# Local attention with its probabilities normalised before the transposition, and its output produced already transposed

## The reference, cut to what matters

```python
qkv = x @ Wqkv; q, k, v = split into 16 heads of 64
q = rotary(l2norm(q) * qs); k = rotary(l2norm(k) * ksc)
# windows of 64 tokens; each sees itself and the window before it: 64 queries x 128 keys
sim = einsum('bhwie,bhwje->bhwij', bq, bk2) * 8.0
sim = where(mask, -max, sim)
attn = softmax(sim, -1)
out = einsum('bhwij,bhwje->bhwie', attn, bv2)
x = x + out.transpose(0, 2, 1, 3).reshape(b, n, 1024) @ Wo
x = x + ffn_layer(x)            # layer norm, 256 -> 2 x 682 with a gelu gate -> 256
```

## Time and profile before

| | |
|---|---|
| median of 3 runs | 5769.8 us (5769.42 to 5777.96) |
| profiled execution | 5762.77 us, its span 5761.5 us |
| mean granted TensorE clock | 0.952 |
| PE busy | 5043.6 us (88%) |
| PEld busy | 3178.3 us (55%) |
| DVE busy | 3618.7 us (63%) |
| ACT busy | 3127.5 us (54%) |
| POOL busy | 2235.3 us (39%) |

### The profile page before, as it was taken

How to read it: one execution, slowest core, us unless ns; L and a number is a source line. 1 busy time by engine, 2 the same in 40 slices (tenths; PEclk the granted TensorE clock), 3 DMA queues, 4 the chain that set the end, 5 groups by cost and what they waited for, 6 DMA issues and landing times.

```text
span 5761.5 us, 93567 instructions
## 1 busy us (share of the span) xinstructions
PE 5043.6 (88%) x36184; PEld 3178.3 (55%) x36184; DVE 3618.7 (63%) x6534; ACT 3127.5 (54%) x6626; POOL 2235.3 (39%) x2178
## 2 busy tenths in 40 slices
PE   5888889978887788877999999999999999999997
PEld 2223333334343343226777777777777777777775
DVE  4655466575665757656766666666666666666664
ACT  2554455433343334446766666666666666666662
POOL 1111001101010110108666666666666666666652
PEclk7999999989898899998999999999999999999998
DMA  4322232221221222211000000000000000000000
GB/s 97 52 48 53 40 56 50 51 52 37 54 40 38 37 50 42 50 20 56 9 16 18 18 21 20 22 16 19 20 16 23 16 22 16 23 16 16 23 9 30
DMA packets 125067, 189.04 MB, mean 33 GB/s; under 512 B 18800, under 2 KB 67568, under 8 KB 124400
## 3 DMA queue, kind: packets, MB, share of 16 engines
q1 hardware_dynamic: 124624, 183.06, 14.4%
HBM read 150.09 MB, written 32.51 MB: 32 GB/s over the span
## 4 chain that ended last, share of the span: by engine, by line
PE 60%; DVE 21%; ACT 10%; issue 6%; DMA 1%; POOL 1%; SPq 0%; DVEq 0%; ACTq 0%; POOLq 0%
PE psum L1206 15%; PE psum L1249 7%; PE psum L465 6%; PE psum L428 4%; PE psum L1250 3%; PE psum L449 3%; DVE maxes L651 3%; ACT probs L831 2%; DVE small_stats L1406 2%; PE psum L410 2%; ACT lprobs L1518 2%; PE psum L1258 2%; PE psum L1291 2%; ACT lwork L1493 2%; PE psum L1282 2%
## 5 line engine op out<-in xcount | busy, mean ns | idle before, releaser
L831 ACT ACTIVATE probs<-psum 128x1024 f32<-128x1024 f32 x768 | 766.7, 1019 | 674.9 <-PE psum L449 389.1
L651 DVE TENSOR_REDUCE maxes<-psum 128x1 f32<-128x1024 f32 x512 | 614.7, 1212 | 341.7 <-PE psum L428 337.8
L1393 DVE TENSOR_TENSOR lwork<-psum,rotary 128x512 f32<-128x512 f32 x384 | 265.2, 691 | 797.3 <-ACT lwork L1493 797.2
L1518 ACT ACTIVATE lprobs<-psum,small_stats,stats 128x128 f32<-128x128 f32 x1536 | 578.4, 459 | 334.3 <-DVE small_stats L1410 333.4
L1572 POOL TENSOR_TENSOR stats<-stats,minus_half 128x8 f32<-128x8 f32 x384 | 642.0, 1672 | 32.0
L1568 POOL TENSOR_TENSOR lwork<-lwork 128x512 f32<-128x512 f32 x384 | 492.2, 1282 | 368.5 <-DVE lwork L1395 364.4
L428 PE MATMUL psum<-stack 96*128 96x512 bf16 x1536 | 486.2, 400 | 152.7 <-ACT probs L831 121.5
L449 PE MATMUL psum<-stack 98*128 98x512 bf16 x1536 | 522.7, 396 | 107.1 <-DVE maxes L651 57.3
L930 POOL TENSOR_TENSOR attn<-attn,sums 128x512 f32<-128x512 f32 x48 | 60.8, 1267 | 1319.1 <-DVE sums L684 1319.1
L1493 ACT ACTIVATE lwork<-psum 128x512 f32<-128x512 f32 x384 | 232.1, 604 | 433.6 <-PE psum L1250 432.9
L1249 PE MATMUL psum<-wqkv_hi,xs_hi 128*128 128x512 f32 x768 | 345.8, 450 | 117.8 <-DVE att_lo L1424 73.5
(11 more groups left out here) (227 smaller groups left out, 12629.2 us busy)
## 6 DMA issues: line engine op xcount, KB each, us to landing
stack<-k_parts SPq DMA_DIRECT2D x288, 128.0 KB
staged<-in_quads SPq DMA_DIRECT2D x144, 256.0 KB, 2.5
k_parts<-parts SPq DMA_DIRECT2D x48, 384.0 KB, 2.8
stack<-q_parts SPq DMA_DIRECT2D x288, 64.0 KB
staged<-in_w SPq DMA_DIRECT2D x54, 256.0 KB, 2.7
ctx<-in_ctxT SPq DMA_DIRECT2D x24, 512.0 KB, 4.8
q_parts<-parts SPq DMA_DIRECT2D x24, 384.0 KB, 2.8
arena<-in_ctxT SPq DMA_DIRECT2D x8, 512.0 KB, 4.5
```

The lines of the kernel that those rows point to most:

```text
L651: ins = vector.tensor_reduce(to, pair(("M", u)), AX.XY, ALU.max)
L831: scalar.activation(probs[:, i % 6, :, :], pair(("E", u)), ACT.Exp).then_inc(S_["E_act"], 1)
L1518: ins = scalar.activation(pr[:, h, :], scores(u)[:, h % 2, h // 2, :], ACT.Exp, bias=st[:, 4 + h:5 + h], scale=y[:, h:h + 1])
```

## The change

Sums of the exponentials are taken by ScalarE while it makes them (`accum_out`). A new stage `nm` (lag 5) takes their reciprocals and multiplies the probabilities on VectorE, before they are turned. `pt` moves to lag 6 and `pv` to lag 7. In `pv` the values are now the weights and the turned probabilities move, so that features come out on the partitions, two heads of a pair in the two halves; `ot` and `heads_out` are gone, and ScalarE and VectorE split `pv`'s bank into `att_hi` and `att_lo`. The column of ones is gone. The maxima are written to PSUM, beside the scores, and read there. `probs` has 3 buffers, `vals` 7, `mixed_vals` 8.

```diff
-        for stage, lag in (("qkv", 0), ("rot", 1), ("tr", 3), ("sc", 4), ("ex", 4), ("pt", 5), ("pv", 6), ("ot", 7)):
+        for stage, lag in (("qkv", 0), ("rot", 1), ("tr", 3), ("sc", 4), ("ex", 4), ("nm", 5), ("pt", 6), ("pv", 7)):
-    rank = {st: i for i, st in enumerate(("wo", "sc", "tr", "rot", "ot", "pv", "ex", "pt"))}
+    rank = {st: i for i, st in enumerate(("wo", "sc", "nm", "tr", "rot", "pv", "ex", "pt"))}
...
                     for h in range(4):
+                        pair, e = h // 2, h % 2
                         for w in range(2):
-                            ins = tensor.matmul(bank(("pv", u, 0))[64 * w:64 * w + 64, h * (LHD + 1):(h + 1) * (LHD + 1)],
-                                                pt[:, h, 64 * w:64 * w + 64], (va if w else vm)[:, h, :], start=True, stop=True)
+                            ins = tensor.matmul(bank(("pv", u, 0))[64 * e:64 * e + 64, pair * P + 64 * w:pair * P + 64 * w + 64],
+                                                (va if w else vm)[:, h, :], pt[:, h, 64 * w:64 * w + 64], start=True, stop=True)
...
-                elif stage == "ot":
-                    PE.wait_ge(S_["pv_dve"], at_("pv", u))
-                    left(one, ("ot", u, 0), PE)
-                    o = heads_out[:, out_at["o", u][0], :, :].rearrange("p (j e) d -> p j (e d)", j=2)
-                    for pair in range(2):
-                        ins = tensor.transpose(bank(("ot", u, 0))[:, tok(pair)], o[:, pair, :], ident[:, :])
...
-                    step(vector.tensor_reduce(st[:, 0:4].rearrange("p (e j) -> p e j", e=2), scores(u), AX.X, ALU.max))
+                    top = psum[:, two[u][0], 2 * P:2 * P + 4].rearrange("p (e j) -> p e j", e=2)
+                    step(vector.tensor_reduce(top, scores(u), AX.X, ALU.max))
                     step.join()
...
-                    vector.scalar_tensor_tensor(out=by_half(st[:, 4:8]), in0=st[:, 0:4].rearrange("p (e j) -> p e j", e=2), scalar=-1.0,
+                    vector.scalar_tensor_tensor(out=by_half(st[:, 4:8]), in0=top, scalar=-1.0,
                                                 in1=by_half(y), op0=ALU.mult, op1=ALU.mult).then_inc(S_["sc_dve"], 1)
+                elif stage == "nm":
+                    rc, pr = soft(u)[:, 8:12], probs[:, prob_at["p", u][0], :, :]
+                    V.wait_ge(S_["ex_act"], at_("ex", u))
+                    step(vector.reciprocal(rc, rc))
+                    step.join()
+                    vector.tensor_tensor(pr, pr, bc(rc, 2, P), ALU.mult).then_inc(S_["nm_dve"], 1)
                 elif stage == "pv":
-                    step(vector.reciprocal(rc.rearrange("p (h d) -> p h d", d=1), ps[:, :, LHD:LHD + 1]))
-                    step.join()
-                    vector.tensor_tensor(heads_out[:, out_at["o", u][0], :, :], ps[:, :, 0:LHD], bc(rc, 2, LHD),
-                                         ALU.mult).then_inc(S_["pv_dve"], 1)
-                elif stage == "ot":
-                    V.wait_ge(S_["ot_act"], at_("ot", u))
-                    vector.tensor_tensor(att_lo[:, :, tok(tt)], wide(bank(("ot", u, 0))[:, 0:2 * P]), att_hi[:, :, tok(tt)].bitcast(F32),
-                                         ALU.subtract).then_inc(S_["ot_dve"], 1)
+                    V.wait_ge(S_["pv_act"], at_("pv", u))
+                    vector.tensor_tensor(att_lo[:, :, tok(tt)], wide(bank(("pv", u, 0))[:, 0:2 * P]), att_hi[:, :, tok(tt)].bitcast(F32),
+                                         ALU.subtract).then_inc(S_["pv_dve"], 1)
...
-                        ins = scalar.activation(pr[:, h, :], scores(u)[:, h % 2, h // 2, :], ACT.Exp, bias=st[:, 4 + h:5 + h], scale=y[:, h:h + 1])
+                        ins = scalar.activation(pr[:, h, :], scores(u)[:, h % 2, h // 2, :], ACT.Exp, bias=st[:, 4 + h:5 + h], scale=y[:, h:h + 1],
+                                                accum_out=st[:, 8 + h:9 + h])
```

More of the change, by code:

```diff
@@ L1111, in last_part @@
         keys = psb("keys", [P, 1, C, 9 * WIN])
-        vals, mixed = psb("vals", [P, 6, 4, LHD + 1]), psb("mixed_vals", [P, 7, 4, LHD + 1])
+        vals, mixed = psb("vals", [P, 7, 4, LHD]), psb("mixed_vals", [P, 8, 4, LHD])
         queries = psb("queries", [P, 1, C, P])
@@ L1116, in last_part @@
         hid_hi, hid_lo = psb("hid_hi", [P, HT, S], F32R), psb("hid_lo", [P, HT, S], F32R)
-        probs = psb("lprobs", [P, 2, 4, P])
+        probs = psb("lprobs", [P, 3, 4, P])
         turned = psb("turned", [P, 2, 4, P])
-        heads_out = psb("heads_out", [P, 2, 4, LHD])
         work = psb("lwork", [P, 9, S])
@@ L1124, in last_part @@
         ln_stats = psb("ln_stats", [P, 2, QT])
-        ONE = {"qkv": 2, "tr": 1, "pt": 1, "pv": 1, "ot": 1, "wo": 2, "fa": 1, "fb": 1, "fy": 1, "fh": 2, "fw": 1}
-        LEAVES = {"qkv": ("qkv_dve", "qkv_act"), "tr": ("tr_act",), "pt": ("pt_act",), "pv": ("pv_dve",), "ot": ("ot_dve",), "wo": ("add_dve", "add_dve"),
+        ONE = {"qkv": 2, "tr": 1, "pt": 1, "pv": 1, "wo": 2, "fa": 1, "fb": 1, "fy": 1, "fh": 2, "fw": 1}
+        LEAVES = {"qkv": ("qkv_dve", "qkv_act"), "tr": ("tr_act",), "pt": ("pt_act",), "pv": ("pv_dve",), "wo": ("add_dve", "add_dve"),
                   "fa": ("fa_dve",), "fb": ("fb_dve",), "fy": ("fy_dve",)}
@@ L1153, in last_part @@
         key_at = use(1, [("tr", 3, [(0,)], ["kT"])], [("sc", 3, [(QT - 1,)], ["kT"], "sc_pe")])
-        val_at = use(6, [("qkv", 4, any_, ["v"])], [("pv", 4, any_, ["v"], "pv_pe")])
-        mix_at = plan(order, range(7),
+        val_at = use(7, [("qkv", 4, any_, ["v"])], [("pv", 4, any_, ["v"], "pv_pe")])
+        mix_at = plan(order, range(8),
                       lambda p: [p[1][:3] + (tt,) for tt in range(QT) if tt == p[1][3] + 1 or tt == p[1][3] == 0] if p[0] == "qkv" else [],
@@ L1165, in last_part @@
         stat_at = use(6, [("qkv", 4, any_, ["norm"])], [("ex", 4, any_, ["norm"], "ex_act")])
-        soft_at = use(4, [("sc", 4, any_, ["soft"])], [("pv", 4, any_, ["soft"], "pv_dve")])
+        soft_at = use(4, [("sc", 4, any_, ["soft"])], [("nm", 4, any_, ["soft"], "nm_dve")])
         stage_at = plan(order, range(2), lambda p: [p] if p[0] == "lq" else [], lambda p: [(p, "lq_pool")] if p[0] == "lq" else [])
@@ L1229, in window_keys @@
             return bass.AP(part.tensor, part.offset, [dims[0], [(odd - even) * WIN, 2], [1, WIN]])
-        def with_one(ap, lo=0, hi=P):
-            return ap[lo:hi, :, 0:LHD]
         def tensor_program():
@@ L1277, in tensor_program @@
                 elif stage == "pt":
-                    PE.wait_ge(S_["ex_act"], at_("ex", u))
+                    PE.wait_ge(S_["nm_dve"], at_("nm", u))
                     left(one, ("pt", u, 0), PE)
@@ L1359, in vector_program @@
             vector.memset(keys[:, :, :, 4 * WIN:5 * WIN], 0.0)
-            vector.memset(mixed[:, :, :, :], 1.0)
-            vector.memset(vals[:, :, :, :], 1.0)
+            vector.memset(mixed[:, :, :, :], 0.0)
             vector.memset(minus_half[:, :], -0.5).then_inc(S_["zeroed"], 1)
@@ L1524, in scalar_program @@
                                       ACT.Copy).then_inc(S_["pt_act"], 1)
-                elif stage == "ot":
+                elif stage == "pv":
                     d, g, b, tt = u
-                    A.wait_ge(S_["ot_pe"], at_("ot", u))
+                    A.wait_ge(S_["pv_pe"], at_("pv", u))
                     if tt == 0 and (d, g, b) != (0, 0, 0):
                         A.wait_ge(S_["add_pe"], order.nth["wo", u[:3]] - 1)
-                    scalar.activation(att_hi[:, :, tok(tt)], wide(bank(("ot", u, 0))[:, 0:2 * P]), ACT.Copy).then_inc(S_["ot_act"], 1)
+                    scalar.activation(att_hi[:, :, tok(tt)], wide(bank(("pv", u, 0))[:, 0:2 * P]), ACT.Copy).then_inc(S_["pv_act"], 1)
                 elif stage == "fa":
```

12 lines of the change are left out of this document (3 added, 9 removed).

## The result

The changed kernel takes 5675.93 us in the median of 4 runs (5672.02 to 5677.29), the kernel before 5769.69 beside it: a ratio of 0.9833, with a 95% interval of 0.9816 to 0.985. So it is faster by 1.7%, some 94 us. The profiled span is 5674.6 us, with a mean granted clock of 0.954.

What follows compares the result with a forecast made beforehand. PE leads (466 of 500 us), with short turns set by a chain through ACT and DVE. Terms sum to -7.6 us a 32-turn pattern, times 12: -91, from 5762.8 to 5672, plus 7: 5680 us, forecast's own range 5630 to 5720.

Steps and rivals of the forecast that it cites:

- 12 turns that PE fills, and the `fy`: Turns filled by PE (6 `fh`, 4 `fw`, `fa`, `fb`): each 0.22 us shorter without two transposes, -2.6 us a pattern.
- 2 turns behind an `fh` that end with `wo`: `qkv` no longer waits for `att_lo`, and `wo` waits until 5.5 us against 7.1: -1.5 each, -3.0 us.
- 4 others behind an `fh`: Set by exponentials, 6.79 us to 6.0: -0.8 in three, the fourth stays, -2.4 us a pattern.
- 4 turns whose `wo` waits for `att_lo`: `att_lo` comes later behind `nm` on DVE: 0.6 in two, 0.9 in one, 0.1 in one, +2.2 us.
- 2 turns behind a `wo`: Turns of 4.80 us, filled by PE with ACT ahead, go to 4.5: -0.6 us a pattern.
- further short turns: Two turns where L1410 lost 1.12 us: -0.6 us; six others set by the exponentials: about -0.1 each, -0.6 us.
- Transposes and `pv`: On PE, removing two transposes of `ot` gains 0.22 us a turn; `pv`'s eight products take 0.62 us again.
- rival 1: `pv` loses its overlap between array halves: 0.39 us in some 14 turns of 32, 65 us, giving 5745; chance 0.12.
- Banks: PSUM banks dealt out again, so the 73.5 us in which `qkv` waits for `att_lo` go; what is late next decides.
- L1410: DVE's subtraction, 743 ns in the median, takes 0.16 us with maxima in PSUM: exponentials start 0.58 us earlier.
- The exponentials: On ACT, four exponentials with their sums take 1.93 us against 1.50: +0.43 us a tile, bounds 0 and 1.15.
- Rival 3: Accumulator reads on ACT don't overlap: exponentials take 1.15 us more, not 0.43, giving 5801, slower than before; chance 0.12.

Runs made afterwards that it cites:

- max_in_sbuf: The changed kernel with the maxima kept in SBUF again: 5832.6 us, 1.0120 of the kernel before.
- before_max_psum: The kernel before with one edit alone, the maxima written to PSUM and read there: 5636.6 us, 0.9779 of the kernel before.
- no_product: The changed kernel without VectorE's product of probabilities and reciprocals, sums and reciprocals kept, so without normalisation: 5588.1 us, 0.9713 of the kernel before.

## Why the prediction held

The forecast of 5680 us came 4 us from the result, and the sum can be held against the trace turn by turn. These are the differences of the median lengths of each of the 32 turns of the pattern, over its 12 times, from the starts of `sc` in both traces, added up by the prediction's own groups:

| group | predicted, us | measured, us |
|---|---|---|
| 12 turns that PE fills, and the `fy` | -2.6 | -3.3 |
| 2 turns behind an `fh` that end with `wo` | -3.0 | -4.1 |
| 4 others behind an `fh` | -2.4 | -3.2 |
| 4 turns whose `wo` waits for `att_lo` | +2.2 | +2.2 |
| 2 turns behind a `wo` | -0.6 | +0.2 |
| further short turns (those of the earlier trace rows among them) | -1.2 | +0.1 |
| together | -7.6 | -8.0 |

The further short turns were 8 in the prediction and are 6 here, since the `fy` is counted in the first row and one `fb` in the fourth, with the turn behind it. Medians needn't add up to the whole: from the first start of `sc` to the last it is 3028.6 us before and 2939.9 after, 7.4 us less for each of the 12. Three groups gained more than forecast and two less. That these misses cancel, so that the total is 4 us off, is luck; most of the chains themselves were read rightly.

The prediction had no term for the clock, and the clock is in these differences. Here are a turn behind an `fh` with `wo` at its end at the lower clock, the like turn of the earlier trace rows, and the first one's counterpart after (us, then busy PE, PEld, DVE, ACT, POOL, and the granted clock):

```profile
3634.76:3646.22 11.46, 9.42 (x73) 7.41 (x72) 8.73 (x18) 7.40 (x18) 8.02 (x8) 0.85 0.07 24
```

```profile
3895.15:3905.17 10.02, 7.86 (x72) 6.11 (x72) 8.25 (x18) 7.40 (x18) 7.36 (x7) 1.00 0.18 56
```

```profile
3618.34:3626.64 8.30, 7.68 (x71) 5.90 (x70) 7.42 (x16) 7.65 (x22) 5.63 (x6) 1.00 0.10 34
```

A clock of 1.00 is 2.4 GHz through the whole stretch; 0.85 means that it stood at 1.2 GHz for a part of it. In the first of these turns it falls at 3640.0, where PE has just stood waiting 1.44 us for `att_lo`. Before, the clock fell in 10 of the 24 turns of this kind, each 1.2 to 1.5 us longer for it, and in 5 of 12 of another turn behind an `fh` (8.34 against 6.78 us); after, in none of these. These differences add up to some 21 us of the 94; the 11 turns after in which the clock still falls take an estimated 7 of them back. The second group would be near -3.0 without it. The clock held up better where PE waited less: its mean is 0.949 in max_in_sbuf, 0.954 in the changed kernel and 0.958 in before_max_psum. But no run separates the two, so the prices of the experiments hold what the clock gave or took.

In the fourth group two large differences cancel. The turn of `fb` is 2.03 us shorter (8.50 us at a clock of 0.81 before, 6.38 at 1.00 after), and the one behind it, which ends with `wo`, 2.04 longer. The longer one is at 1.00 after:

```profile
3334.19:3344.66 10.47, 8.39 (x73) 6.34 (x72) 7.06 (x16) 6.59 (x22) 9.21 (x11) 1.00 0.13 46
```

In it PE waits 1.28 us before `fy` for POOL's `ln_stats`, and 0.80 before `wo` for `att_lo`. The first is a wait that the prediction set at nothing: it reckoned that blocking POOL changes no term, as POOL has time to spare. That wait of `fy` is 12.4 us in all, and 2.0 in no_product.

- **Transposes and `pv`.** From `tr` to `pv` it is 0.586 us, where `tr` to `ot` and `ot` to `pv` were 0.492 and 0.312 in the median: 0.22 less, as predicted. `pv` itself was taken at 0.62 and is 0.664; its overlap isn't lost, as rival 1 had it (1.0), and two products on one half in a row cost 0.05 us in all. The two halves still run side by side against the order of the code: the compiled kernel keeps that order, with the four records of two products on one half ahead of those on the other, yet the first two of a `pv`, one of each half, start 0.01 us apart (3345.92 and 3345.93). So the rule of the Trainium skill that the prediction cited ("TensorE: Matmul & The Clock Gate", part 3, "The mechanism") doesn't hold here either.
- **Turns that PE fills.** Those with `fh` or `fw` gained 0.24 to 0.37 us, not 0.22. The step "12 x -0.22" lacked a term: the 512-column products of `fh` and `fw` are 1.5 to 2% shorter because their moving tiles now start at a multiple of 64 bytes. The parts close: in a turn with `fh` 0.22 less for the transposes, 0.05 more for `pv` and 0.12 less for `fh` make 0.29, as measured, and with `fw` 0.22, 0.05 and 0.07 make 0.24. The addresses are worth about 20 us and have nothing to do with attention.
- **Banks.** The 73.5 us are gone, and "what is late next decides" was right. But L1384 was not on my list of what is late next. The wait for it grew by 29 us, 23 of them in the turns of the last group, and this is most of the 25 us by which the last two groups fell short (2.1 a pattern). What dealing out the banks anew is worth by itself no run isolates; the maxima alone already bring the 73.5 us down to 43.5. In the turn of these groups that lost most (+0.96 us in the median) ACT makes `xn_hi` only after the now longer exponentials and `turned` (L1511); DVE's `xn_lo` waits for that, and the rotary products stand behind `xn_lo`. One of these turns starts at 3349.28 (timeline of ACT, DVE and PE):

```profile
3348.71 0.61 ACT L1511 ACTIVATE turned<-psum 128x512 f32<-128x512 f32 x1
...
3349.19 1.35 ACT L1531 ACTIVATE xn_hi<-lwork,vecs 128x512 fp32r<-128x512 f32 x2
...
3350.57 1.67 DVE L1441 SCALAR_TENSOR_TENSOR xn_lo<-lwork,vecs,xn_hi 128x512 fp32r<-128x512 f32 x2 [1.97 <-ACT xn_hi L1531]
...
3353.10 0.41 DVE L1384 TENSOR_TENSOR lwork<-psum,rotary 128x256 f32<-128x256 f32 x1
...
3353.56 0.50 PE L1245 MATMUL psum<-wqkv_hi,xs_hi 128*128 128x512 f32 x1 [1.70 <-DVE lwork L1384]
```

`xn_lo` starts 1.29 us into the turn; in the same turn of the kernel before it was 0.70 (3359.89 less 3359.19).

- **L1410** became 163 ns (0.16 predicted). **The exponentials** take 1.87 us (1.93 predicted). **The product** has a mean of 1007 ns in the profile (0.68 plus 0.3 predicted), and the chain from L1400 to the end of `att_lo` is 2.20 us (2.2 predicted). Turns behind an `fh` are 5.6 to 5.9 us and, with `wo`, 8.0 to 8.4 (6.0 and 8.5 predicted).

What the prediction didn't see is how the parts stand to each other. It summed by turns and never asked what each edit would bring alone. Rival 3 was the nearest: the sums do cost 54 us, through the wait of `sc` that it named, and the product costs 69, mostly through the wait of `wo`. Only the maxima in PSUM, which the prediction treated as one term among several, outweigh both. Of the 127 us that they bring alone the change keeps 96, although it also has the aligned tiles and no transposes. The single prices don't add up to the whole, because a turn is set by whichever wait ends last; so I give no price for the missing transposes in the whole, which no run isolates. The Trainium skill ("SBUF — State Buffer", "SBUF: two separate sides") says that DVE and POOL exclude each other when the DVE instruction has two SBUF inputs and POOL's reads SBUF. With that max_in_sbuf and before_max_psum agree: 745 and 163 ns in the median for the same four elements.

## What to carry to other kernels

When a small instruction on VectorE takes several times its least duration, look at what POOL does beside it and at where its operands lie, before changing the algorithm: here one operand moved to PSUM gave 127 us, and the restructuring around it cost 31 of them. Test each part of a bundle alone; a bundle that gains can hide a part that loses. And before a gain is put down to an edit, look at stages whose instructions the edit left alone: if they changed too, compare the tiles' addresses and the granted clock of those turns.

## What the runs showed of the hardware

- An fp32r product whose moving tile starts 32 bytes past a multiple of 64 is slower than one at a multiple: 396 against 389 ns for the record of 512 columns, and 5.68 against 5.56 us for the 24 products of a turn's two `fh`. It was shown both ways, by adding 32 bytes to the kernel before and by taking the changed kernel off the multiple: the kernels at a multiple are the shorter ones, those at 32 past it the longer. Only the starts of the tiles behind the values were moved; which of them matters, and whether other offsets differ, wasn't tried.
- A read of the accumulator takes 0.20 us, but most of it lies beside the next exponential: four exponentials go from 1.50 to 1.87 us, about 0.09 us a read.
- Two SBUF operands on DVE and POOL's work hold up each other, not DVE alone: POOL's L1556 has a mean of 1477 ns with the product beside it and 1286 without.
